# Tiles of the fourth sweep that also serve the fifth sweep, the fifth sweep's chunk order turned, and two constants issued first

## The reference

```python
# x: (4096, 128), adj: (4096, 4096), all float32
def L0(x, adj):  agg = adj @ x + beta[:, None] * x
                 return (1 / (adj.sum(1) + beta))[:, None] * agg @ kernel + bias
def L1(x, adj):  h = relu(adj @ (x @ W1) + b1)        # 20 columns
                 h = relu(adj @ (h @ W2) + b2)        # 20 columns
                 h = relu(adj @ (h @ W3) + b3)        # 128 columns
                 return relu(h + x)
def L2(x, adj):  s = 1 / (sqrt(adj.sum(1)) + 1e-8)
                 return (adj * s[:, None] * s[None, :]) @ (x @ W + b)
def L3(H, adj):  S = (H @ W_l) @ (H @ W_r).T
                 return adj @ H + gamma * (softmax(S) @ H @ W_h @ W_g)
for L in (L0, L1, L2, L3):
    x = layernorm(x + L(x, adj))
```

## Time and profile before

| | us |
|---|---|
| median of 3 runs (1359.14 to 1367.57) | 1361.51 |
| the profiled execution | 1359.1 |
| its span | 1357.3 |
| TensorE (PE) busy | 1291.2 |
| VectorE (DVE) busy | 929.9 |
| ScalarE (ACT) busy | 716.5 |
| GpSimd (POOL) busy | 255.3 |

### The profile page before, as it was taken

The page is one execution under the profiler, slowest core; times in us unless marked ns, Lnnn a source line. Parts: engine busy times, 40 slices in busy tenths (PEclk is TensorE's granted clock), DMA queues, the critical chain, the costliest instruction groups (busy, mean ns, idle before and its releaser), DMA issues.

```text
span 1357.3 us, 17259 instructions
## 1 busy us (share of the span) xinstructions
PE 1291.2 (95%) x5911; PEld 795.1 (59%) x5911; DVE 929.9 (69%) x1213; ACT 716.5 (53%) x880; POOL 255.3 (19%) x167
## 2 busy tenths in 40 slices
PE   8799999998999988899999999999899999999987
PEld 3344444433333232588888788887567767767764
DVE  5466665561000164799999988886988888878885
ACT  0211010112111032588888777776788788787785
POOL 0111001100000011001010100005243343344345
PEclk9899999998999999999999999999999999999999
DMA  9586655553979989899999999990000000000000
GB/s 374 203 338 247 234 224 207 205 203 131 369 302 377 359 285 407 300 358 374 375 380 376 333 356 360 385 355 0 1 1 0 1 1 1 0 18 15 0 1 31
DMA packets 81087, 288.01 MB, mean 212 GB/s; under 512 B 9466, under 2 KB 11130, under 8 KB 81018
## 3 DMA queue, kind: packets, MB, share of 16 engines
q1 hardware_dynamic: 78768, 286.30, 55.6%
q10 hardware_dynamic: 2250, 0.82, 0.2%
HBM read 284.98 MB, written 2.10 MB: 212 GB/s over the span
## 4 chain that ended last, share of the span: by engine, by line
PE 69%; DVE 13%; issue 6%; ACT 5%; DMA 3%; ACTq 1%; SPq 1%; POOL 1%; DVEq 0%; POOLq 0%
PE acc L1256 14%; PE acc L1324 8%; PE acc L1445 7%; DVE t_lo L989 7%; PE acc L1363 4%; PE acc L1358 4%; PE acc L1359 4%; DMA raw<-in_adj_s 2%; PE rs L1264 2%; PE acc L1435 2%; PE acc L1436 2%; PE acc L1439 2%; PE rs L1329 2%; PE e L1400 2%; PE e L1402 2%
## 5 line engine op out<-in xcount | busy, mean ns | idle before, releaser
L989 DVE TENSOR_TENSOR t_lo<-raw,t_hi 128x1024 fp32r<-128x1024 f32 x256 | 307.4, 1243 | 23.9 <-ACT t_hi L711 18.9
L711 ACT ACTIVATE t_hi<-raw 128x1024 fp32r<-128x1024 f32 x256 | 262.8, 1055 | 39.5 <-PE acc L1363 37.8
L1358 PE MATMUL acc<-t_hi,st_hi 128*128 128x512 f32 x512 | 202.5, 396 | 2.4 <-ACT t_hi L711 2.0
L1359 PE MATMUL acc<-t_hi,st_lo 128*128 128x512 f32 x512 | 199.6, 390 | 0.0
L584 POOL TENSOR_TENSOR ring_lo<-ring,p_hi 128x1024 fp32r<-128x1024 f32 x64 | 155.4, 2428 | 220.4 <-ACT p_hi L765 220.3
L1256 PE MATMUL acc<-raw,x 128*128 128x512 f32 x400 | 179.8, 598 | 0.0
L1363 PE MATMUL acc<-t_lo,st_hi 128*128 128x512 f32 x512 | 159.9, 393 | 5.3 <-DVE t_lo L989 5.0
L1063 DVE TENSOR_TENSOR ring<-ring,e 128x1024 f32<-128x1024 f32 x128 | 153.9, 1211 | 0.1
L759 ACT ACTIVATE ring<-ring 128x1024 f32<-128x1024 f32 x128 | 134.2, 1054 | 25.0 <-DVE ring L1063 24.9
L1256 PEld LDWEIGHTS acc<-raw,x 128*128 128x128 f32 x400 | 74.0, 191 | 92.3 <-issue 92.3
L556 POOL COPY x<-xn 128x512 f32<-128x512 f32 (+1 forms) x24 | 20.7, 864 | 565.0 <-ACT xn L652 565.0
(11 more groups left out here) (214 smaller groups left out, 1878.1 us busy)
## 6 DMA issues: line engine op xcount, KB each, us to landing
raw<-in_adj_s SPq DMA_DIRECT2D x506, 512.0 KB, 5.8
kept_t<-in_adj_s SPq DMA_DIRECT2D x8, 512.0 KB, 7.4
x<-in_x SPq DMA_DIRECT2D x4, 512.0 KB, 10.2
kept_x<-in_adj_s SPq DMA_DIRECT2D x4, 512.0 KB, 6.6
kept_e<-in_adj_s SPq DMA_DIRECT2D x4, 512.0 KB, 7.6
kept_l<-in_adj_s SPq DMA_DIRECT2D x4, 512.0 KB, 7.2
kept_s<-in_adj_s SPq DMA_DIRECT2D x4, 512.0 KB, 7.0
kept_v<-in_adj_s SPq DMA_DIRECT2D x4, 512.0 KB, 7.3
```

The source lines that it names most:

```text
L711: nc.scalar.activation(t_hi[:, g % HL, :], raw[:, k, :], ACT.Copy).then_inc(hi_done, 1)
L989: nc.vector.tensor_tensor(t_lo[:, k, :], raw[:, slot_no(s, c, g), :], t_hi[:, k, :].bitcast(F32), ALU.subtract).then_inc(lo_done, 1)
L1358: mm(a[:, :], block_of(st_hi, b), hi[:, m], start=(g == 0 and j == 0), stop=False)
L1359: mm(a[:, :], block_of(st_lo, b), hi[:, m], start=False, stop=False)
```

## The change

The fourth sweep's pairs (chunk 2 with blocks 7 and 6; chunk 1 with 7, 6, 5; chunk 0 with 7, 6, 5, 4), nine pairs or 18 ring tiles, are also split and multiplied for the fifth sweep, within the fourth. TensorE does the narrow product of both tiles of a pair, then the wide ones, into `ahead`. The splits stand in ScalarE's and VectorE's programs between the steps of the epilogue. The fifth sweep leaves these tiles out: its chunks 2, 1 and 0 have 12, 10 and 8 tiles; it runs the chunks downwards, and the sixth sweep starts its first chunk with block 7. The part sums of chunks 2, 1 and 0 are stored by ScalarE and added by VectorE, which evacuates those chunks of the fifth sweep in ScalarE's place. Some steps of the epilogue stand one tile earlier. At the start ident and beta are issued before everything else on ScalarE's queue, the other 16 constants once part 1 of x has landed; GpSimd and TensorE wait only for the first two until chunk 0's epilogue.

```diff
--- before.py
+++ after.py
...
@@ -61,7 +61,9 @@
...
-ORDER = (tuple(range(NC)), tuple(reversed(range(NC))), tuple(range(NC)), tuple(reversed(range(NC))))
+UP, DOWN = tuple(range(NC)), tuple(reversed(range(NC)))
+ORDER = (UP, DOWN, UP, DOWN, DOWN)
+WIDE_EARLY = {2: (7, 6), 1: (7, 6, 5), 0: (7, 6, 5, 4)}
...
@@ -71,11 +73,13 @@
 def row(s, r):
-    return ORDER[s][r] if s in FLAT else r
+    return ORDER[s][r] if s < S5 else r
 def joined(s, c, d):
+    if s == S3:
+        return d in WIDE_EARLY.get(c, ())
...
@@ -95,15 +99,19 @@
...
     else:
-        last = [d for d in (c + 1, c - 1, c) if d in mine and d in KEPT[c]]
-        if s == 1:
+        last = [d for d in (c + 1, c - 1, c) if d in mine and d in KEPT[c] and s < S4]
+        if s == 1 or s == S4:
             mine.reverse()
+        if s == S3 and c in WIDE_EARLY:
+            joint = list(WIDE_EARLY[c])
+            others = [d for d in mine if d not in joint]
+            mine = others + joint if c == max(WIDE_EARLY) else joint + others
...
 def plan():
     items, seq = {}, 0
-    for s in FLAT:
+    for s in range(S5):
...
@@ -298,30 +309,58 @@
         def wide_no(s, c, g):
-            return c * NG + ((s - S4) * NC * NG + g)
+            return WIDE_NO[s, c, g] if s < S5 else c * NG + (len(WIDE) + g)
         def tile_no(s, c, g):
-            return T_WIDE + wide_no(s, c, g)
+            return ITEMS[s, c][g].seq if s < S5 else c * NG + (T_WIDE + g)
+        def length(s, c):
+            return len(ITEMS[s, c]) if s < S5 else NG
         def group_no(s, c, g):
-            return NG - 1 - g if s == S4 and first(c) else g
+            if s == S4:
+                return 2 * ITEMS[s, c][g].d + ITEMS[s, c][g].h
+            return (NG - 1 - g) ^ 1 if first(c) else g
         def slot_no(s, c, g):
-            return (T_WIDE + g) % RAW
+            return (tile_no(s, c, g) if s < S5 else T_WIDE + g) % RAW
+        def split_slot(s, c, g):
+            return (wide_no(s, c, g) if s < S5 else len(WIDE) + g) % HL
         def landed(s, c, g):
-            return c * (16 * NG // RAW) + 16 * ((T_WIDE + (s - S4) * NC * NG + g) // RAW + 1)
+            if s < S5:
+                return 16 * (tile_no(s, c, g) // RAW + 1)
+            return c * (16 * NG // RAW) + 16 * ((T_WIDE + g) // RAW + 1)
+        def place(pos, s, c):
+            return min(pos, length(s, c) - 1)
         def wait_slot(sp, s, c, g):
             if s == S4 and first(c) and g < RAW:
-                sp.wait_ge(pe_tile, T_WIDE - RAW + g + 1)
+                sp.wait_ge(pe_tile, tile_no(s, c, g) - RAW + 1)
...
                 sp.wait_ge(lo_done, wide_no(s, c, g) - (RAW - 1))
+        def wait_split_slot(eng, s, c, g):
+            if s == S5:
+                eng.wait_ge(pe_tile, tile_no(s, c, g) - (HL - 1))
+                return
+            m = wide_no(s, c, g) - HL
+            if m < 0:
+                eng.wait_ge(pe_acc, S3 * NC + ORDER[S3].index(3) + 1)
+            else:
+                q, r, n = WIDE[m]
+                eng.wait_ge(pe_tile, tile_no(q, r, n) + 1)
...
@@ -419,7 +458,8 @@
...
-        consts = [(ident, ident_in), (comb, comb_in), (k0, w["L0_gnn_kernel"]), (w1, w["L1_gnn_W1"]),
+        consts_first = [(ident, ident_in), (beta, beta_in)]
+        consts = [(comb, comb_in), (k0, w["L0_gnn_kernel"]), (w1, w["L1_gnn_W1"]),
...
@@ -447,11 +487,15 @@
...
             else:
-                eng.wait_ge(S["xw"], done("xw", 4, d))
+                eng.wait_ge(S["xw"], done("xw", 4, ORDER[S4].index(d)))
         def stationary_no(s, d):
-            return ORDER[3].index(d) + 1 if s == S4 else NC + d + 1
+            return ORDER[3].index(d) + 1 if s == S4 else NC + ORDER[S4].index(d) + 1
+        def adds_store(s, c):
+            return s in NARROW or s == S4 and stored(S3, row(s, c)) > 0
...
@@ -502,10 +546,10 @@
...
                     return
-                for g in range(NG):
+                for g in range(length(s, c)):
...
                     k = slot_no(s, c, g)
-                    sp.dma_start(raw[:, k, :], tile(c, group_no(s, c, g))).then_inc(raw_in[k], 16)
+                    sp.dma_start(raw[:, k, :], tile(row(s, c), group_no(s, c, g))).then_inc(raw_in[k], 16)
...
@@ -516,7 +560,7 @@
...
         def _(pool):
-            pool.wait_ge(const_in, n_const)
+            pool.wait_ge(first_in, 16 * len(consts_first))
...
@@ -533,6 +577,8 @@
...
                 alone(pool)
+                if s == 0 and first(c):
+                    pool.wait_ge(const_in, n_const)
...
@@ -602,24 +648,25 @@
             def stationary_hi(s, d):
                 if s == S5:
-                    act.wait_ge(pe_tile, tile_no(S4, NC - 1, 2 * d + 1) + 1)
+                    last = max(i.seq for r in range(NC) for i in ITEMS[S4, r] if i.d == d)
+                    act.wait_ge(pe_tile, last + 1)
...
             def evacuate(s, c, par):
-                if s in NARROW:
+                if adds_store(s, c):
...
                 else:
-                    act.wait_ge(pe_tile, tile_no(s, c, NG - 1) + 1)
+                    act.wait_ge(pe_tile, tile_no(s, c, length(s, c) - 1) + 1)
...
             def store_ahead(s, r):
-                if (s, r) not in STORES:
+                if s > S3 or (s, r) not in STORES:
...
@@ -683,41 +730,52 @@
...
                     return
+                wide = [n for n, i in enumerate(ITEMS[S3, r]) if i.fused]
...
                         transposed(3, q)
+                for n in wide[:2]:
+                    split_hi(S3, r, n)
                 deviation(3, pr)
+                for n in wide[2:4]:
+                    split_hi(S3, r, n)
                 normalise(3, pr)
+                for n in wide[4:]:
+                    split_hi(S3, r, n)
...
                     transposed(3, r - 1)
+                store_ahead(3, pr)
...
                     stationary_hi(S4, row(3, r - 3))
+            def split_hi(s, c, g):
+                k = slot_no(s, c, g)
+                act.wait_ge(raw_in[k], landed(s, c, g))
+                wait_split_slot(act, s, c, g)
+                nc.scalar.activation(t_hi[:, split_slot(s, c, g), :], raw[:, k, :], ACT.Copy).then_inc(hi_done, 1)
             def step(s, c, par):
...
                 ps, pc = before(s, c)
-                early = 3 if s == S4 and first(c) else 0
-                for g in range(NG):
+                early = 3 if s == S4 and first(c) else 1
+                for g in range(length(s, c)):
...
                     if s == S5 and first(c) and g % 2 == 0:
-                        stationary_hi(S5, g // 2)
-                    k = slot_no(s, c, g)
-                    act.wait_ge(raw_in[k], landed(s, c, g))
-                    if not (s == S4 and first(c) and g < HL):
-                        act.wait_ge(pe_tile, tile_no(s, c, g) - (HL - 1))
-                    nc.scalar.activation(t_hi[:, g % HL, :], raw[:, k, :], ACT.Copy).then_inc(hi_done, 1)
-                    if g == 2:
+                        stationary_hi(S5, group_no(s, c, g) // 2)
+                    split_hi(s, c, g)
+                    if g == (0 if s == S4 and first(c) else 2):
                         evacuate(ps, pc, 1 - par)
+                        store_ahead(ps, pc)
...
                         second(ps, pc)
-                    if g == 8 - early:
+                    if g == place(8 - early, s, c):
                         deviation(ps, pc)
-                    if g == 10 - early:
+                    if g == place(10 - early, s, c):
                         normalise(ps, pc)
-                    if g == 12 - early:
+                    if g == place(12 - early, s, c):
...
@@ -733,7 +791,9 @@
...
-            act.wait_ge(x_in[XP - 1], 16)
+            for dst, src in consts_first:
+                nc.scalar.dma_start(dst[:, :], src).then_inc(first_in, 16)
+            act.wait_ge(x_in[1], 16)
...
@@ -845,10 +905,13 @@
             def evacuate_narrow(s, r):
-                if s not in NARROW:
+                if s == S5 or not adds_store(s, r):
...
                 c = row(s, r)
-                dve.wait_ge(pe_acc, s * NC + r + 1)
+                if s == S4:
+                    dve.wait_ge(pe_tile, tile_no(s, r, length(s, r) - 1) + 1)
+                else:
+                    dve.wait_ge(pe_acc, s * NC + r + 1)
...
@@ -962,33 +1025,45 @@
...
                 if ps == 3:
+                    wide = [n for n, i in enumerate(ITEMS[S3, r]) if i.fused]
                     residual_1(ps, pr)
+                    for n in wide[:1]:
+                        split_lo(S3, r, n)
                     residual_2(ps, pr)
+                    for n in wide[1:2]:
+                        split_lo(S3, r, n)
                     statistics(ps, pr)
+                    for n in wide[2:4]:
+                        split_lo(S3, r, n)
                     scales(ps, pr)
+                    for n in wide[4:]:
+                        split_lo(S3, r, n)
...
                         stationary_lo(S4, row(3, r - 3))
+            def split_lo(s, c, g):
```

(65 more changed lines are left out.)

13 lines of the change are left out of this document (8 added, 5 removed).

## The result

The changed kernel takes 1374.57 us (median of 7 runs, 1369.91 to 1378.39); the kernel before, run beside it, 1359.14. The ratio is 1.010, with an interval of 1.0078 to 1.0123. The forecast was 1363.2 with a range of 1342 to 1377, so the time lies in the range, but 11 us above the forecast, and the slowdown of 1% is small but clear of the spread. The profiled execution has a span of 1374.3 us against 1357.3: 17.0 to be explained.

The account below looks back on a forecast made before the run. Limits differ by stage: TensorE and nearly VectorE in the fifth sweep, DMA in the fourth's last three chunks. 1359.1 - 9.5 + 32.6 - 24.5 + 1.5 + 4.0 = 1363.2 us; range 1342 to 1377.

Parts of the forecast that it names:

- The sign: Whole kernel: slightly slower, 1363.2 us against 1359.1 on the profiled execution.
- no change: Whole kernel: a time between 1347.9 and 1375.1 us, about 1% either way; chance 0.64 of landing within.
- Start, -9.5: Kernel start: TensorE's 8.7 us wait for bx goes, bx matmuls save 1.0, constants sharing DMA cost 0.2.
- Rival 3: Start gives less: all 3.1 us of the constants' DMA fall on chunk 0's tiles, 1366.1 us; inside the forecast.
- The forecast's 3.1 us: Start: DMA time of the constants over all 16 engines, cited as agreeing that queues interleave on them.
- Fourth sweep, +32.6: Last three chunks grow by 7.9, 11.4 and 13.4 us, from walking three in-order queues with 24.5 us of added TensorE work.
- rival 2: Fourth sweep: clock falls behind the nine joint pairs' waits, 9 x 1.7 = 15.3 us more, 1378.5 us; chance 0.14.
- The bound of +12.1: Fourth sweep's last three chunks if TensorE alone decided: 55.4 us against 43.3.
- rival 1: It hides: TensorE or DMA decides, fourth sweep +12.1 us, no excess in short chunks, 1338.7 us; chance 0.22.
- Fifth sweep, -19.0: 18 tiles fewer save 24.5 us; first chunk costs +1.5, short chunks and the sixth sweep's first chunk +4.0.
- the sentence on the moved hooks: Epilogue steps placed one tile earlier cost nothing in full chunks, where VectorE has 0.8 us to spare.
- VectorE as the limit of the short chunks: Fifth sweep, chunks of 12, 10, 8 tiles: VectorE needs 16.9, 15.2, 12.9 us, TensorE 16.8, 14.1, 11.4; +2.7.

Follow-up runs that it names:

- e1: Kernel before with only the new start (ident and beta first, other 16 constants after part 1 of x): 1351.14 us, ratio 0.993.
- e8: Changed kernel without the 18 joint tiles' splits on ScalarE and VectorE, TensorE multiplying other data without waiting for splits: 1357.9 us, ratio 0.998.
- e4: Changed kernel with the epilogue's steps of the fifth sweep's last chunk one tile earlier on ScalarE and VectorE: 1371.89 us, ratio 1.009.
- e10: Changed kernel without joint tiles, with the fifth and sixth sweeps' epilogue steps back one tile later, as before: 1352.14 us, ratio 0.993.
- e5: Changed kernel, fourth sweep reordered: VectorE's sums, statistics, scales and ScalarE's deviation, normalise before splits (chunks 1, 0: after ScalarE's first four): 1372.8 us, ratio 1.008.
- e6: e5 with two splits ahead for four, joint tiles last in chunks 1 and 0 too, and the steps of e4: 1365.59 us, ratio 1.0035.
- e3: Changed kernel with joint tiles in the fourth sweep's chunk 2 alone (4 tiles): 1359.75 us, ratio 0.998.

## Why the prediction came out as it did

The sign was right and the size was not. On the profiled execution +4.1 us was forecast and +17.0 came: 3.0 of the difference up to the fourth sweep's chunk 2, 3.9 in the fourth sweep, 6.1 in the fifth, less 0.1 behind it. That 1374.57 is just inside what was called no change (1375.1) is luck: this bound is 1% above a median of three runs, 1361.51; 1% above 1359.14, the kernel before as run beside the changed one, is 1372.7. The changed kernel is slower since the work moved to the fourth sweep costs more there (36.5 us) than the fifth sweep gives back (12.9), against a start that gains 8. By steps:

- *Start, -9.5.* The traces show -8.3, e1 shows 9.2 by its trace and about 10 by the medians. Right. In the changed kernel's trace the first tile came at 7.04 for 6.12, and the first 16 matmuls took 9.95 us for 8.82; the two took back 2.0. (The kernel before had lost 0.5 more than was counted, in the 8 records of tiles, partly at half clock, behind its long wait: 4.11 us for 3.60.) In the other ten traces with this start the first matmul is at 6.32 to 6.64, so half of the 0.9 or more is chance; whether the rest is due to the two early constants, one trace of the kernel before can't tell. Rival 3 is out: in e1 chunk 0's tiles lose nothing beyond the later first matmul. The forecast's 3.1 us is a share of the engines' time and doesn't show that queues interleave; the changed kernel does, where from 10 to 25 us the constants' queue took 8.9% and the tiles' queue 95.0% of the same 16 engines.
- *Fourth sweep, +32.6: measured +36.5.* Chunk 1 and chunk 0 were followed well: +11.5 and +14.2 for +11.4 and +13.4, with the waits in the forecast's order. Chunk 2 took +10.8 for +7.9. The walk had the order right (the idle time ahead of the third epilogue step from 515 to 520 is the 4.4 us seen) but kept the clock at 2.4 GHz. That was left to rival 2, and the fall cost 2.2 us at most. Rival 2 was thus right for one wait in the fourth sweep; the others there, of 0.5 to 1.7 us, let nothing fall. Two more falls of 3.4 us came outside it, behind waits of 2.02 and 2.57 us; TensorE was busy throughout both, so they cost up to 1.7 us each. The clock was a term of 2 us in the fourth sweep and 5 or 6 in all, and not 0 or 15.
- *How the +32.6 was read was wrong.* The forecast had about 20 us of TensorE idle time in it, and 12.1 of TensorE's own work. There were 13.9 us idle, and by e8 some 19 are TensorE's own work.
- *The bound of +12.1, rival 1, was wrong.* It was built from the paces of narrow tiles and three epilogues, 30.9 us of TensorE's work. The earlier trace rows had the better number: 13.80 + 12.29 + 13.48 = 39.6 us busy of 43.3, which leaves 3.7 us of cover for 24.5 of work, so +20.8. e8 measured +19.6. (Busy time in a stretch that waits for DMA is not all work: with 24.5 us of work added it rose by 21.7, to 61.2.) The chunks at a DMA share of 1.01 looked like an idle TensorE, and it was 91% busy. My sum had left out that chunk 2 turns two earlier chunks (transposes at 507.03 and 514.01; the second costs 1.7 us) and chunk 1's wait of 0.9 us for the copy; what makes up the rest, perhaps the short matmuls beyond their count, no run separates. Rival 1's chance of 0.22 should have been near nothing.
- *Fifth sweep, -19.0: measured -12.9.* This is the term that was mis-sized most; 1.3 of the loss it allowed for was to come in the sixth sweep's first chunk, which took 26.2 us for 26.3. The first chunk came at +3.2 for +1.5: besides ScalarE's wait for VectorE's copy, the clock fell for 3.4 us behind it (582.8 to 586.2). The last chunk, with 8 tiles, took 17.5 us where VectorE's work came to 12.9: the sentence on the moved hooks said nothing of the short chunks, where deviation and normalise are pushed behind the last split and hold the next sweep's first. Moving them (e4) took 2.3 off this chunk and put 1.2 on the next; at 15.2 us it was still 2.3 above the 12.9, with VectorE busy for 13.7. Full chunks took 22.5 for 22.2, a quarter of a microsecond each or a little more, which is gone with the steps back in their place (e10); the forecast had put that at nothing.
- *VectorE as the limit of the short chunks* was right in kind: 17.1 and 15.4 us for the 16.9 and 15.2 forecast, with VectorE busy for 16.1 and 14.8 of them.

What I had thought to be the cause afterwards, the order in the queues, is a part only. The two experiments that changed it (e5, e6) gained 2 and 9 us where 17 and 27 were expected. In the one place followed up, four split slots and products done by pairs turned the removed wait into another; how much of e6's rest is that, I didn't separate. Of the 6.8 us that e3 loses with two pairs, the traces show 6.0: its chunk 2 had the same gap and fall, one more fall of the clock came in chunk 1, and the fifth sweep gave back 1.0 less than its tiles are worth.

## What to carry to other kernels

A stage that waits for DMA is cover only for the idle time that the engine has there: read its busy time in the stage (91% here) before moving work into it, and not only the DMA's share. Check also that the stage the work is taken from gets shorter by as much: here it gave back 13 of 24.5 us, since its first chunk got longer and its short chunks did not shorten with their tiles. Work split over three in-order queues needs room in all three, between whose steps it is put; a run like e8, which left two of the three out, is a cheap test of whether the move can pay at all. When a loop is cut short, steps placed by its count pile up at its end and hold what follows.
